# A fused attention and ternary feed-forward block: a second buffer for P's 512-column tiles, AV one slot later, and ternary weights cast by GpSimd's transfers

## The chip, the cores and the metric

The kernel runs on one core of one Trainium2 chip. The metric is the device time of one execution in microseconds (us). The kernel before was timed three times; its profile comes from one further execution.

## The reference

The input x has 16 batches of 512 rows and 512 columns, in float32. Attention and feed-forward work side by side on the same normalised rows:

```python
xn = layernorm(x)                                   # over the 512 columns
# attention, 16 heads of 32
qkv = xn @ w_qkv.T + b_qkv                          # 1536 x 512 weights
scores = q @ k.T / sqrt(32) + causal mask
out = softmax(scores) @ v
attn = out @ w_out.T + b_out
# feed-forward, 1408 hidden columns, ternary weights (-1, 0, 1)
g = (xn @ gate_w.T) * gate_s
u = (xn @ up_w.T) * up_s
ffn = ((silu(g) * u) @ down_w.T) * down_s
result = x + attn + ffn
```

## The kernel before

All products run in fp16. A float32 value that needs more precision is split in two fp16 parts, a high part and the rest ("low"), and the products of the parts are summed. The ternary weights are exact in fp16 and have one part.

**Slots.** The heads are worked on in groups of four (G, 64 groups in all, four to a batch b). A group has U = 10 slots, so a batch has 40 and the whole run has 640, numbered n. A slot has one unit of scores: one head's 512-column tile of query rows (units 0, 1, 5, 6), or two smaller tiles. Each engine has its own program, a list in this order of slots, and takes its instructions strictly in that order. What is to be done in a slot besides the scores stands in tables: `av_at`, `qk_at`, `v_at`, `o_at`, `d_at`, `f_at`, `norm_at`.

**A unit's path.** TensorE writes the scores to one of four PSUM banks in slot n (`scores`). VectorE masks them and takes the maximum (`maximum`, L588). ScalarE takes the exponential (`exponent`, L500). Two slots later ScalarE writes the high part of P (`high`, L492), and VectorE the low part (`low`, L598), both to a buffer `phl[qt]` that is chosen by the tile's width, 128(qt+1) columns. `scores(n)` waits for `low(n-4)`, since it takes the same bank. SyncE then transposes the buffer to `pt` by a DMA (`turn_p`, L954); there is one such DMA for each half p of a group (heads 0 and 1, heads 2 and 3) and each width, eight in a group. `high` of a tile waits for the transposition of the previous contents of its buffer (`d_pt[qt]`). There is one buffer for each width, so the 512-column tiles of slots 5 and 6 wait for the transposition of slots 0 and 1, which SyncE starts in slot 5.

**AV.** `av(G)` has 48 products of the transposed P with v. It stands in slot 4 of the next group, behind that slot's scores (`av_at`, AV_K = 4). It waits for all eight transpositions. ScalarE drains it one slot later to `q32[0]` (`drain_av`, L468); GpSimd splits that to the two parts of `att` (`split_av`, L791 and L793; in GpSimd's list of a slot it stands ahead of `residual`, `down_add`, `split_hidden` and `load_xin`). After a batch's last group the four products with w_out follow: `o(b, t)` in slots 47, 48, 49 and 51 counted from the batch's first slot, that is, slots 7, 8, 9 and 11 of the next batch. They wait for `p_al`, the end of `split_av`.

**Feed-forward.** `gate_up(f)` writes a tile of g and u to one bank; ScalarE, VectorE (L608, L613) and GpSimd (`split_hidden`, L804, L808, L810) make the hidden tile of it. There are 22 a batch; `F_WIN` says in which slots. The first group of a batch (but for batch 0) has them in slots 2, 2, 4 and 5. `down_product` runs in slots 19, 21, 37, 39; VectorE scales its result to `dtmp` (L632), GpSimd adds that to `res` (L820).

**Weights before.** `w_qkv` comes in 12 chunks, the ternary gate, up and down in 33 (11 each). Each chunk is 128 x 512 float32, 256 KB. SyncE issues all 45 as plain DMAs to 15 staging slots that lie in buffers not yet in use (`res`, `att`, `xnT[1]`, parts of `ht`, `dtmp`), by a planner: `slot_of`, `w_load`, `w_slot`. ScalarE (17 ternary chunks, L434) or GpSimd (16, L764) copies a chunk to fp16. 18 chunks are issued ahead of the first slot and the others in the first 20 slots, in SyncE's queue between `stack` and `turn_p`.

**Normalisation.** GpSimd loads a tile of x to `xin` (L838) four slots ahead of its statistics (L562). VectorE scales it to `xs32` (L572), GpSimd takes the high part (L908), VectorE the low part (L737).

Of the kernel before, what the change touches and what calls it, by code (L numbers as in the profile page):

```python
# [5 lines left out]
ACT = mybir.ActivationFunctionType  # L6
# [21 lines left out]
U = 10  # L28
# [38 lines left out]
def fast_path(nc, ctx, B, x, w_qkv, b_qkv, w_out, b_out, gate, up, down, gate_s, up_s, down_s, out):  # L67
# [33 lines left out]
    phl = [sb(f"phl{i}", [128, 2, 2, 128 * (i + 1)], F16) for i in range(4)]  # L101
# [22 lines left out]
    d_w = [sem(f"d_w{i}") for i in range(15)]  # L124
# [4 lines left out]
    d_pt = [sem(f"d_pt{i}") for i in range(4)]  # L129
# [16 lines left out]
    AV_K, QK_K = 4, (3, 6)  # L146
# [15 lines left out]
    av_at = {U * (G + 1) + AV_K: G for G in range(NGRP)}  # L162
# [13 lines left out]
    later = [(n - 4, ("norm", *v)) for n, v in norm_at.items()] + [(n - 3, ("check", c)) for n, c in check_at.items()]  # L176
    for n, what in sorted(later + [(n - 3, ("wout", k)) for n, k in wout_at.items()]):
        i = what[-1] % 2
        xin_load_at[n] = what
        xin_turn[what] = 1 + sum(x[-1] % 2 == i for x in xin_turn)  # L180
        xin_free[what] = xin_reader[i]
        xin_reader[i] = {"norm": (v_xs, 4 * what[1] + what[-1] + 1), "check": (a_ms, what[1] + 1), "wout": (v_wo, what[1] + 1)}[what[0]]
# [36 lines left out]


    pair = lambda t, i: t[:, 2 * i:2 * i + 2, :].rearrange("p a b -> p (a b)").bitcast(F32)
    stage = [(res[i][:, :], 16 + i) for i in range(4)]
    stage += [(pair(att[:, i // 2], i % 2), 15) for i in range(4)]
    stage += [(pair(xnT[1], i), 8) for i in range(4)]
    stage += [(x0[2], 15), (x0[3], 20), (dtmp[:, :], 20)]
    flat = lambda w: w.rearrange("p a b -> p (a b)")
    chunks, w_slot = [], []

    def qkv_chunk(n, m):
        chunks.append(("split", ("wqkv", m), w_qkv[m], flat(wqkv[:, 0, m]), flat(wqkv[:, 1, m])))  # L230
        w_slot.append(n)

    def gate_up_chunks(n, i):
        chunks.append(("act", ("wg", i), gate[i], flat(wg[:, i]), None))
        chunks.append(("pool", ("wu", i), up[i], flat(wu[:, i]), None))
        w_slot.extend((n, n))

    def down_chunk(n, i):
        chunks.append(("pool" if i % 2 else "act", ("wd", i), down[i], wd[:, i], None))
        w_slot.append(n)  # L240

    for m in (8, 9, 0, 4, 1, 5, 10, 11):
        qkv_chunk(-1, m)
    gate_up_chunks(-1, 0)
    qkv_chunk(-1, 2)
    qkv_chunk(-1, 6)
    for n, i in ((-1, 1), (1, 2), (2, 3), (4, 4), (5, 5), (6, 6), (8, 7)):
        gate_up_chunks(n, i)
    qkv_chunk(9, 3)
    gate_up_chunks(10, 8)  # L250
    down_chunk(10, 0)
    qkv_chunk(11, 7)
    gate_up_chunks(12, 9)
    down_chunk(12, 1)
    gate_up_chunks(13, 10)
    for n, i in ((13, 2), (13, 3), (14, 4), (14, 5), (15, 6), (15, 7), (16, 8), (16, 9), (18, 10)):
        down_chunk(n, i)
    W_FIRST, W_EARLY = w_slot.index(1), 18
    NCH = len(chunks)
    slot_of, before = [], []  # L260
    for n in range(NCH):
        last = lambda i: max([m for m in range(n) if slot_of[m] == i], default=-1)
        free = [i for i in range(len(stage)) if stage[i][1] > w_slot[n] and (n >= 12 or i < 12)]
        slot_of.append(min(free, key=lambda i: (last(i), i)))
        before.append(last(slot_of[n]))
    turn_of = [slot_of[:n].count(slot_of[n]) for n in range(NCH)]
    slot_last = [max(n for n in range(NCH) if slot_of[n] == i) for i in range(len(stage))]
    stage = [buf for buf, n in stage]
    w_load = [max([w_slot[n] - 4, 0] + [w_slot[before[n]] + 1] * (before[n] >= 0)) for n in range(NCH)]


    on_act = [sum(c[0] != "pool" for c in chunks[:n + 1]) for n in range(NCH)]
    on_pool = [sum(c[0] == "pool" for c in chunks[:n + 1]) for n in range(NCH)]
    lows = [sum(c[0] == "split" for c in chunks[:n + 1]) for n in range(NCH)]
    finished = [{"split": (v_w, lows[n]), "act": (a_w, on_act[n]), "pool": (p_w, on_pool[n])}[c[0]] for n, c in enumerate(chunks)]
    ready = {c[1]: finished[n] for n, c in enumerate(chunks)}
# [8 lines left out]
    def tensor_program(eng):  # L285
# [42 lines left out]
        def av(G):  # L328
            b, g = divmod(G, 4)
            for qt in range(4):  # L330
                w.wait_ge(d_pt[qt], 16 * (2 * G + 2))
# [95 lines left out]
    def scalar_program(eng):  # L427
        w = Waits(eng)

        def weight(n):  # L430
            kind, key, src, hi, lo = chunks[n]
            if kind != "pool":
                w.wait_ge(d_w[slot_of[n]], 16 * (turn_of[n] + 1))
                eng.activation(hi, stage[slot_of[n]], ACT.Copy, scale=WS if kind == "split" else 1.0).then_inc(a_w, 1)  # L434
# [42 lines left out]
        def high(n):  # L477
# [5 lines left out]
            for j, qt, off in segs(u):  # L483
                w.wait_ge(d_pt[qt], 16 * (2 * G + j // 2))
# [5 lines left out]
            for k, (j, qt, off) in enumerate(segs(u)):  # L490
                c, W = 2 * (n % NSTAT) + k, 128 * (qt + 1)
                i = eng.activation(phl[qt][:, j % 2, 0], pb[:, off:off + W], ACT.Copy, scale=st_r[:, c:c + 1])  # L492
# [11 lines left out]
        for t in range(4):  # L504
            hl = xhl[t][:, 0] if t < 2 else phl[3][:, t - 2, 0]
# [8 lines left out]
        for n in range(8, 11):  # L514
            weight(n)
        drain_qk(0, 1)
        weight(11)
        v_high(0, 0, 1)
        for n in range(12, W_FIRST):
            weight(n)  # L520
# [4 lines left out]
        for n in range(LAST):  # L525
# [16 lines left out]
            for i in range(W_FIRST, NCH):  # L542
                if w_slot[i] == n:
                    weight(i)


    def vector_program(eng):
        w = Waits(eng)

        def weight_low(n):  # L550
            kind, key, src, hi, lo = chunks[n]
            if kind == "split":
                w.wait_ge(a_w, on_act[n])
                eng.scalar_tensor_tensor(lo, stage[slot_of[n]], WS, hi, ALU.mult, ALU.subtract).then_inc(v_w, 1)  # L554
# [13 lines left out]
        def scaled(i, t, xs, xi):  # L568
            st = lst[t]
            w.wait_ge(v_xl, i if i > 4 else 0)  # L570
            w.wait_ge(p_rs, i + 1)
            eng.tensor_scalar(xs, xi, st[:, 6:7], st[:, 8:9], op0=ALU.subtract, op1=ALU.mult).then_inc(v_xs, 1)  # L572
# [20 lines left out]
        def low(n):  # L593
            pb = bank[n % NSB]
            w.wait_ge(a_hi, n + 1)
            for k, (j, qt, off) in enumerate(segs(n % U)):
                c, W = 2 * (n % NSTAT) + k, 128 * (qt + 1)
                i = eng.scalar_tensor_tensor(phl[qt][:, j % 2, 1], pb[:, off:off + W], st_r[:, c:c + 1], phl[qt][:, j % 2, 0],  # L598
# [16 lines left out]
        def v_low(b, hf, tp):  # L615
            psum = job_bank["v", b, hf, tp][:, :].rearrange("p (a f) -> p a f", a=2)
            part = lambda p: vv[:, p, 2 * tp:2 * tp + 2, 256 * hf:256 * hf + 256]
            w.wait_ge(a_vh, 4 * b + 2 * hf + tp + 1)
            eng.scalar_tensor_tensor(part(1), psum, QS / (XS * WS), part(0), ALU.mult, ALU.subtract).then_inc(v_vl, 1)
# [7 lines left out]
        def down_scale(b, t):  # L627
            w.wait_ge(p_set, 9)
            w.wait_ge(*finished[slot_last[14]])
            w.wait_ge(p_dy, 4 * b + t)  # L630
# [605 lines left out]
```

## Time and profile before

| | |
|---|---|
| median of 3 runs | 1947.92 us (1947.15 to 1948.87) |
| profiled execution | 1948.99 us, with a span of 1947.2 us |
| TensorE busy (matmul) | 1866.0 us, 96% of the span |
| VectorE, ScalarE, GpSimd busy | 1504.4, 1450.8, 1255.8 us |
| mean granted TensorE clock | 0.99 of full speed |

The span runs from the first instruction to the last. An engine's busy time is a union of its instructions, so a matmul that is queued behind another counts once. "L588" is line 588 of the kernel before. PE is TensorE, DVE VectorE, ACT ScalarE, POOL GpSimd; SPq is SyncE's queue of DMA issues. All of TensorE's products have one line, L287, so they are told apart by their tiles (`bank<-pt,vv` is AV, `bank<-wout,att` the product with w_out, `bank<-stk` the scores).

### The profile page before, as it was taken

What the parts mean: (1) busy time and instruction counts of PE and PEld (TensorE: products, weight loads), DVE (VectorE), ACT (ScalarE), POOL (GpSimd) and SP (SyncE); (2) the same over time, 40 slices, a digit from 0 to 9 for tenths busy, and PEclk for the clock granted to TensorE, in tenths of its full rate; (3) what the DMA queues carried; (4) which work ended last, traced back from release to release, by engine and by line L of the source; (5) the groups of instructions that cost most, each with busy time, mean ns of one, the idle gap of its engine ahead of it and who ended that gap; (6) DMA issues with size and microseconds to landing.
All of it is one profiled execution on the core that took longest, in us unless ns stands there. A gap on an engine that the chain in (4) does not pass through costs nothing.

```text
span 1947.2 us, 44190 instructions
## 1 busy us (share of the span) xinstructions
PE 1866.0 (96%) x14978; PEld 1222.0 (63%) x14978; DVE 1504.4 (77%) x4516; ACT 1450.8 (75%) x4280; POOL 1255.8 (64%) x1800
## 2 busy tenths in 40 slices
PE   6689999999999999999999999999999999999997
PEld 4456566665766666566666756666566666756663
DVE  4677778777787877878778787877878777787884
ACT  4677687867778787787877778777787777777683
POOL 4676666857577585776857576575666656576462
PEclk9899999999999999999999999999999999999998
DMA  7997978889798796978889798786968878797674
GB/s 217 216 171 141 185 134 182 159 151 184 134 191 144 159 182 127 205 139 170 166 144 193 136 178 138 156 168 122 198 129 169 144 142 175 135 187 129 122 157 94
DMA packets 818839, 310.26 MB, mean 159 GB/s; under 512 B 756464, under 2 KB 789232, under 8 KB 818608
## 3 DMA queue, kind: packets, MB, share of 16 engines
q1 hardware_dynamic: 800928, 249.44, 70.9%
q0 software_dynamic: 17680, 57.95, 10.4%
q8 instruction: 119, 1.95, 0.4%
q14 instruction: 112, 0.92, 0.2%
HBM read 55.59 MB, written 16.78 MB: 37 GB/s over the span
## 4 chain that ended last, share of the span: by engine, by line
PE 70%; DVE 9%; DMA 6%; SPq 6%; ACT 5%; issue 3%; POOL 2%; POOLq 0%; ACTq 0%; DVEq 0%
PE bank L287 70%; DMA pt<-phl 5%; SPq L947 4%; DVE phl L598 3%; ACT phl L492 2%; DVE bank L588 1%; SPq L954 1%; ACT bank L500 1%; DVE res L625 1%; DVE small L562 1%; DVE xhl L737 1%; ACT small L488 0%; SPq L939 0%; DMA xnT<-in_up_dram 0%; DVE ft L608 0%
## 5 line engine op out<-in xcount | busy, mean ns | idle before, releaser
L598 DVE SCALAR_TENSOR_TENSOR phl<-bank,small,phl 128x512 f16<-128x512 f32 (+3 forms) x1024 | 526.6, 546 | 187.9 <-ACT phl L492 184.9
L500 ACT ACTIVATE bank<-bank,small 128x512 f32<-128x512 f32 (+3 forms) x1024 | 516.0, 505 | 167.2 <-DVE small L588 166.4
L588 DVE CUSTOM_DVE_ANT_0 bank<-bank,mask 128x512 f32<-128x512 f32 (+3 forms) x1024 | 484.3, 504 | 162.8 <-PE bank L287 160.4
L492 ACT ACTIVATE phl<-bank,small 128x512 f16<-128x512 f32 (+3 forms) x1024 | 500.0, 531 | 91.6 <-DMA pt<-phl 81.0
L287 PE MATMUL bank<-xnT,wg 128*128 128x256 f16 x2816 | 367.8, 273 | 6.5 <-DVE fh L613 4.8
L287 PE MATMUL bank<-xnT,wu 128*128 128x256 f16 x2816 | 367.4, 274 | 0.0
L287 PE MATMUL bank<-xnT,wqkv 128*128 128x512 f16 x1536 | 352.4, 379 | 1.1 <-ACT q L461 1.1
L287 PE MATMUL bank<-wd,ht 128*128 128x512 f16 x1408 | 317.5, 381 | 4.0 <-POOL ht L810 2.1
L287 PEld LDWEIGHTS bank<-xnT,wg 128*128 128x128 f16 x2816 | 264.0, 98 | 68.9 <-issue 5.9
L287 PEld LDWEIGHTS bank<-xnT,wu 128*128 128x128 f16 x2816 | 276.6, 98 | 33.0
L287 PE MATMUL bank<-stk 96*128 96x512 f16 (+3 forms) x1024 | 245.8, 301 | 26.6 <-DVE phl L598 25.2
L810 POOL TENSOR_TENSOR ht<-fh,ht 128x256 f16<-128x256 f32 x352 | 238.4, 677 | 29.4
L287 PEld LDWEIGHTS bank<-xnT,wqkv 128*128 128x128 f16 x1536 | 147.8, 98 | 167.2 <-issue 1.7
L804 POOL TENSOR_TENSOR fh<-fh,ft 128x256 f32<-128x256 f32 x176 | 127.6, 725 | 188.9 <-DVE ft L608 188.8
L287 PEld LDWEIGHTS bank<-wd,ht 128*128 128x128 f16 x1408 | 137.2, 98 | 162.8 <-issue 4.1
L450 ACT ACTIVATE ft<-bank,small 128x256 f32<-128x256 f32 x352 | 169.6, 483 | 77.8 <-PE bank L287 77.6
L808 POOL TENSOR_SCALAR ht<-fh 128x256 f16<-128x256 f32 x352 | 143.2, 407 | 130.6 <-DVE fh L613 114.1
L500 ACT ACTIVATION_READ_ACCUMULATOR bank<-bank,small 128x1 f32 x1024 | 216.0, 211 | 0.0
L287 PE MATMUL bank<-wqkv,xnT 128*128 128x256 f16 x1536 | 180.6, 275 | 14.1 <-DMA xnT<-xhl 14.1
L820 POOL TENSOR_TENSOR res<-res,dtmp 128x512 f32<-128x512 f32 x64 | 81.1, 1268 | 155.7 <-DVE dtmp L632 155.5
L287 PE MATMUL bank<-wout,att 128*128 128x512 f16 x768 | 177.5, 381 | 3.7 <-POOL att L793 2.9
L287 PEld LDWEIGHTS bank<-wqkv,xnT 128*128 128x128 f16 x1536 | 150.4, 98 | 38.9 <-DVE wqkv L554 14.0
(110 smaller groups left out, 2195.6 us busy)
## 6 DMA issues: line engine op xcount, KB each, us to landing
stk<-qkp SPq DMA_DIRECT2D x768, 64.0 KB, 2.1
res<-in_x_dram POOLq DMA_DIRECT2D x64, 256.0 KB, 4.7
xin<-in_x_dram POOLq DMA_DIRECT2D x60, 256.0 KB, 4.6
out_dram<-res POOLq DMA_DIRECT2D x60, 256.0 KB, 3.7
pt<-phl SPq DMA_TRANSPOSE x512, 4.2
xin<-in_gate_dram POOLq DMA_DIRECT2D x11, 256.0 KB, 3.5
xin<-in_up_dram POOLq DMA_DIRECT2D x11, 256.0 KB, 3.3
xin<-in_down_dram POOLq DMA_DIRECT2D x11, 256.0 KB, 3.5
```

Source lines behind the costliest of these rows:

```text
L287: mm = lambda o, lhs, rhs, start, stop, **k: eng.matmul(o, lhs, rhs, start=start, stop=stop, skip_group_check=True, **k)
L450: eng.activation(ft[f % 3][:, :], bank[4 + f % 2][:, 0:256], ACT.Tanh, scale=gsh[:, k:k + 1]).then_inc(a_ft, 1)
L492: i = eng.activation(phl[qt][:, j % 2, 0], pb[:, off:off + W], ACT.Copy, scale=st_r[:, c:c + 1])
L500: i = eng.activation(pb[:, off:off + W], pb[:, off:off + W], ACT.Exp, bias=st_m[:, c:c + 1], scale=-1.0, accum_out=st_s[:, c:c + 1])
L562: eng.bn_stats(st[:, 0:6], xi).then_inc(v_bn, 1)
L588: i = eng.tensor_tensor_reduce(out=bk[:, off:off + W], in0=bk[:, off:off + W], in1=mask[:, 512 - W:512], scale=-(32.0 ** -0.5) / (QS * QS) ...
L598: i = eng.scalar_tensor_tensor(phl[qt][:, j % 2, 1], pb[:, off:off + W], st_r[:, c:c + 1], phl[qt][:, j % 2, 0], ALU.mult, ALU.subtract)
L804: eng.tensor_tensor(hh[:, :], hh[:, :], ft[f % 3][:, :], ALU.mult).then_inc(p_fm, 1)
L808: eng.tensor_scalar(hs[:, 0], hh[:, :], 1.0, 1.0, op0=ALU.mult, op1=ALU.mult).then_inc(p_hh, 1)
L810: eng.tensor_tensor(hs[:, 1], hh[:, :], hs[:, 0], ALU.subtract).then_inc(p_fl, 1)
L820: eng.tensor_tensor(res[t][:, :], res[t][:, :], dtmp[:, :], ALU.add).then_inc(p_dy, 1)
L947: eng.dma_start(stk[G % 2][32 * blk:32 * blk + 32, j], qkp[G % 2][32 * j:32 * j + 32, a:a + step + 1:step, :]).then_inc(d_stk[2 * (G % 2) ...
```

## The change

Three edits are made together.

1. `phl[3]` becomes two buffers, one for each half of a group, each with its own semaphore (`d_pt[3][p]`). `high` of a 512-column tile now waits for the transposition of the same half of the group before. AV_K goes from 4 to 5 (the last group's AV stays in slot 4), and `turn_p(G, 0, 3)` from slot 5 to slot 6 of SyncE's list.
2. The ternary weights are no longer staged. GpSimd issues 15 DMAs that read float32 and write fp16 straight into `wg`, `wu` and `wd`: two of one chunk, ten of two chunks, three of three or four chunks. Six of them come as soon as the fourth tile of batch 0's x is transposed (`d_xT[3]`), ahead of `split_qk(0, 0)`; two behind `split_qk(0, 1)`; four behind `split_qk(1, 1)`; the three of `wd` in slots 1, 3 and 5. The copies on ScalarE and GpSimd are gone. All 12 chunks of w_qkv are now loaded and split ahead of slot 0.
3. To make room, `dtmp` becomes `q32[0]`, the buffer to which AV is drained, with two new waits (`drain_av` for earlier `down_add`, `down_scale` for earlier `split_av`); `xs32` is gone and the scaled tile stays in `xin`, so that `xin` is free two slots later, and its loads are issued three slots ahead of the statistics in place of four.

```diff
-    phl = [sb(f"phl{i}", [128, 2, 2, 128 * (i + 1)], F16) for i in range(4)]
+    phl = [[sb(f"phl{i}", [128, 2, 2, 128 * (i + 1)], F16)] for i in range(3)]
+    phl.append([sb(f"phl3_{p}", [128, 2, 2, 512], F16) for p in range(2)])
...
-    dtmp = sb("dtmp", [128, 512], F32)
+    dtmp = q32[0]
-    xs32 = sb("xs32", [128, 512], F32)
...
-    AV_K, QK_K = 4, (3, 6)
+    AV_K, QK_K = 5, (3, 6)
...
-    av_at = {U * (G + 1) + AV_K: G for G in range(NGRP)}
+    av_at = {U * (G + 1) + (AV_K if G < NGRP - 1 else 4): G for G in range(NGRP)}
+    avs_ahead = {bt: sum(n < m for n in av_at) for m, bt in d_at.items()}
+    ds_ahead = {G: sum(n < m for n in d_at) for m, G in av_at.items()}
...
-    later = [(n - 4, ("norm", *v)) for n, v in norm_at.items()] + ...
+    later = [(n - (4 if n < 4 else 3), ("norm", *v)) for n, v in norm_at.items()] + ...
...
+    chunks = (8, 9, 0, 4, 1, 5, 10, 11, 2, 6, 3, 7)
+    ffn_loads, ffn_sem = [], {}
+    for lo, hi in ((0, 1), (1, 3), (3, 5), (5, 7), (7, 9), (9, 11)):
+        ffn_loads += [("wg", lo, hi), ("wu", lo, hi)]
+    ffn_loads += [("wd", 0, 4), ("wd", 4, 8), ("wd", 8, 11)]
+    for i, (name, lo, hi) in enumerate(ffn_loads):
+        for k in range(lo, hi):
+            ready[name, k] = (d_ffn[i], 16)
+    ffn_load_at = {1: (12,), 3: (13,), 5: (14,)}
...
         def drain_av(G):
             g = G % 4
             w.wait_ge(p_al, G)
+            w.wait_ge(p_dy, ds_ahead[G])
...
             for j, qt, off in segs(u):
-                w.wait_ge(d_pt[qt], 16 * (2 * G + j // 2))
+                w.wait_ge(*((d_pt[3][j // 2], 16 * G) if qt == 3 else (d_pt[qt][0], 16 * (2 * G + j // 2))))
...
         def down_scale(b, t):
             w.wait_ge(p_dy, 4 * b + t)
+            w.wait_ge(p_al, avs_ahead[b, t])
...
+        def load_ffn(i):
+            name, lo, hi = ffn_loads[i]
+            if name == "wd":
+                dst = wd[:, lo:hi]
+            else:
+                dst = {"wg": wg, "wu": wu}[name][:, lo:hi].rearrange("p k a b -> p k (a b)")
+            eng.dma_start(dst, {"wg": gate, "wu": up, "wd": down}[name][lo:hi].rearrange("k p f -> p k f")).then_inc(d_ffn[i], 16)
...
-        for n in range(10):
-            weight(n)
+        w.wait_ge(d_xT[3], 16)
+        for i in range(6):
+            load_ffn(i)
         split_qk(0, 0)
         split_qk(0, 1)
-        for n in range(10, W_FIRST):
-            weight(n)
+        load_ffn(6)
+        load_ffn(7)
         split_qk(1, 0)
         split_qk(1, 1)
+        for i in range(8, 12):
+            load_ffn(i)
...
-                if k == 5:
-                    turn_p(G, 0, 3, n - 4)
                 if k == 6:
+                    turn_p(G, 0, 3, n - 5)
                     turn_p(G, 0, 2, n - 3)
                     turn_p(G, 0, 0, n - 3)
...
-            for i in range(W_EARLY, NCH):
-                if w_load[i] == n:
-                    load_weight(i)
```

## Rows read from the trace of the kernel before

**Rows 1.** Busy time by stage: stretch, its length, engines, TensorE clock, DMA share, GB/s

```profile
36.60:80.00 43.40, 33.62 (x236) 23.47 (x236) 35.19 (x103) 35.24 (x98) 28.84 (x48) 0.92 0.98 224
80.00:91.14 11.14, 3.32 (x48) 1.89 (x49) 1.12 (x4) 2.47 (x8) 3.38 (x5) 0.55 1.10 214
91.14:130.00 38.86, 34.73 (x253) 21.14 (x250) 25.29 (x75) 26.44 (x76) 28.58 (x37) 0.91 0.92 182
130.00:169.50 39.50, 37.51 (x294) 24.58 (x292) 30.88 (x96) 33.03 (x99) 27.02 (x40) 1.00 0.78 145
...
406.40:1811.30 1404.90, 1386.72 (x11233) 913.04 (x11232) 1112.38 (x3353) 1071.56 (x3182) 932.78 (x1333) 1.00 0.83 158
```

**Rows 2.** Waits of TensorE from 130 to 1860 us: total, times, longest

```profile
PE bank L287 <- DVE phl L598: 17.8, 16, 3.1
PE bank L287 <- issue: 5.5, 8, 1.4
PE bank L287 <- POOL ht L810: 2.1, 3, 1.0
```

**Rows 3.** Waits of TensorE in the first 130 us

```profile
PE bank L287 <- ACT wd L434: 1.9, 1, 1.9
```

**Rows 4.** The chain that ended last, around a stall at 695 us: start, length

```profile
689.06 5.43 DMA pt<-phl
...
696.04 63.96 PE bank L287 x504
```

**Rows 5.** Timeline of TensorE in the head: the first AV

```profile
87.82 3.39 PE L287 MATMUL bank<-pt,vv 128*32 128x512 f16 x48 [11.61 <-DMA pt<-phl]
```

**Rows 6.** Timeline of SyncE's queue ahead of the first AV

```profile
79.75 4.13 SPq L954 DMA_TRANSPOSE pt<-phl  x1
```

**Rows 7.** Timeline, slots 44 to 47: a batch's last AV and first product with w_out

```profile
181.98 1.81 PE L287 MATMUL bank<-pt,vv 128*32 128x512 f16 x48
183.73 1.05 PE L287 MATMUL bank<-xnT,wg 128*128 128x256 f16 x8
...
185.70 1.04 PE L287 MATMUL bank<-xnT,wg 128*128 128x256 f16 x8
...
190.48 1.89 PE L287 MATMUL bank<-wout,att 128*128 128x512 f16 x8
...
186.47 0.69 ACT L468 ACTIVATE q<-bank,small 128x512 f32<-128x512 f32 x1
...
187.19 0.41 DVE L608 SCALAR_TENSOR_TENSOR ft<-ft,bank 128x256 f32<-128x256 f32 x1
...
187.95 1.15 POOL L793 TENSOR_TENSOR att<-q,att 128x512 f16<-128x512 f32 x1
189.06 0.73 POOL L804 TENSOR_TENSOR fh<-fh,ft 128x256 f32<-128x256 f32 x1
...
190.36 0.67 POOL L810 TENSOR_TENSOR ht<-fh,ht 128x256 f16<-128x256 f32 x1
```

**Rows 8.** The same two instructions in the last of the 15 batches that have them

```profile
1829.79 1.16 POOL L793 TENSOR_TENSOR att<-q,att 128x512 f16<-128x512 f32 x1
...
1832.33 1.89 PE L287 MATMUL bank<-wout,att 128*128 128x512 f16 x8
```

**Rows 9.** Durations by line: ns min/median/max

```profile
L434 ACT ACTIVATE wg<-att x4: 635/648/673, 52.7 to 78.0; 128x512 f16<-128x512 f32 x4
...
L838 POOL DMA_DIRECT2D xin<-in_x_dram x60: 584/611/763, 37.4 to 1719.1; - x60
```

**Rows 10.** DMA rate from 20 to 30 us, 40 slices of 0.25 us

```profile
GB/s 90 107 131 90 131 238 262 279 270 238 328 311 320 279 426 402 410 401 402 418 402 393 393 402 401 401 402 393 385 393 393 303 238 246 246 229 164 25 0 0
```

**Rows 11.** The start of the first group: GpSimd, TensorE and the first statistics from `xin`

```profile
19.13 5.61 PE L287 MATMUL bank<-xnT,wqkv 128*128 128x512 f16 x24
...
25.23 0.62 POOL L780 TENSOR_SCALAR qkp<-q 128x512 f16<-128x512 f32 x1
...
47.42 0.61 DVE small L562
```

More of the change, by code:

```diff
@@ L123, in fast_path @@
     d_small = [sem(f"d_small{i}") for i in range(5)]
-    d_w = [sem(f"d_w{i}") for i in range(15)]
+    d_w = [sem(f"d_w{i}") for i in range(12)]
+    d_ffn = [sem(f"d_ffn{i}") for i in range(15)]
     d_x0 = [sem(f"d_x0{i}") for i in range(4)]
@@ L221, in fast_path @@
     pair = lambda t, i: t[:, 2 * i:2 * i + 2, :].rearrange("p a b -> p (a b)").bitcast(F32)
[L222 to L225, printed above, removed]
+    stage = [res[i][:, :] for i in range(4)]
+    stage += [pair(att[:, i // 2], i % 2) for i in range(4)]
+    stage += [pair(xnT[1], i) for i in range(4)]
+    part = lambda qt, j: phl[qt][j // 2 if qt == 3 else 0]
@@ L226, in fast_path @@
     flat = lambda w: w.rearrange("p a b -> p (a b)")
[L227 to L240, printed above, removed]
@@ L258, in fast_path @@
-    W_FIRST, W_EARLY = w_slot.index(1), 18
-    NCH = len(chunks)
[L260 to L275, printed above, removed]
@@ L276, in fast_path @@
-    ready = {c[1]: finished[n] for n, c in enumerate(chunks)}
+    chunks = (8, 9, 0, 4, 1, 5, 10, 11, 2, 6, 3, 7)
+    NCH = len(chunks)
+    ready = {("wqkv", m): (v_w, n + 1) for n, m in enumerate(chunks)}
+    ffn_loads, ffn_sem = [], {}
[5 more added lines that the diff above has]
+            ready[name, k] = (d_ffn[i], 16)
@@ L430, in weight @@
         def weight(n):
[L431 to L434, printed above, removed]
+            w.wait_ge(d_w[n], 16)
+            eng.activation(flat(wqkv[:, 0, chunks[n]]), stage[n], ACT.Copy, scale=WS).then_inc(a_w, 1)
         def wout_high(k):
@@ L504, in scalar_program @@
         for t in range(4):
-            hl = xhl[t][:, 0] if t < 2 else phl[3][:, t - 2, 0]
+            hl = xhl[t][:, 0] if t < 2 else phl[3][0][:, t - 2, 0]
             w.wait_ge(v_xs, t + 1)
@@ L513, in scalar_program @@
         drain_qk(0, 0)
-        for n in range(8, 11):
-            weight(n)
+        weight(8)
         drain_qk(0, 1)
+        weight(9)
+        v_high(0, 0, 1)
+        weight(10)
         weight(11)
-        v_high(0, 0, 1)
-        for n in range(12, W_FIRST):
-            weight(n)
         drain_qk(1, 0)
@@ L687, in first_low @@
         def first_low(t):
-            hl = xhl[t][:, :, :] if t < 2 else phl[3][:, t - 2]
+            hl = xhl[t][:, :, :] if t < 2 else phl[3][0][:, t - 2]
             w.wait_ge(a_xh, t + 1)
@@ L708, in vector_program @@
         v_low(0, 0, 0)
-        for n in range(7, W_FIRST):
+        for n in range(7, 10):
             weight_low(n)
         v_low(0, 0, 1)
+        for n in range(10, 12):
+            weight_low(n)
         for f in range(F_FIRST):
@@ L907, in gpsimd_program @@
                 w.wait_ge(v_xs, i + 1)
-                eng.tensor_scalar(xhl[t % 2][:, 0], xs32[:, :], 1.0, 1.0, op0=ALU.mult, op1=ALU.mult).then_inc(p_xh, 1)
-            for i in range(W_FIRST, NCH):
-                if w_slot[i] == n:
-                    weight(i)
+                eng.tensor_scalar(xhl[t % 2][:, 0], xin[t % 2][:, :], 1.0, 1.0, op0=ALU.mult, op1=ALU.mult).then_inc(p_xh, 1)
+            for i in ffn_load_at.get(n, ()):
+                load_ffn(i)
             if n in xin_load_at:
@@ L932, in turn_x @@
             if b == 1:
[L933 to L934 removed]
+                w.wait_ge(v_w, NCH)
             if b >= 2:
@@ L964, in sync_program @@
         for t in range(4):
-            turn_x(0, t, xhl[t] if t < 2 else phl[3][:, t - 2])
+            turn_x(0, t, xhl[t] if t < 2 else phl[3][0][:, t - 2])
             load_weight(4 + t)
@@ L968, in sync_program @@
             eng.dma_start(dst[:, :], src.to_broadcast([128, 512])).then_inc(d_small[i + 3], 16)
-        for n in range(8, W_EARLY):
+        for n in range(8, NCH):
             load_weight(n)
```

86 lines of the change are left out of this document (25 added, 61 removed).

## The prediction

> **What bounds the kernel now.** I read the stages first, then what TensorE waits for, then the timeline around the longest waits and around the instructions that the change moves.
>
> The stages [rows 1] show two regimes. From 406 to 1811 us, twelve batches, TensorE is busy for 1386.7 of 1404.9 us at a full clock. Nothing but its own work bounds it there, and all that any edit can win in these twelve batches is 18.2 us. A batch takes 117.1 us, a slot 2.93. In the first batch it is otherwise. TensorE idles for 9.8, 7.8, 4.1 and 2.0 us in the four stretches from 36.6 to 169.5 us, 23.7 us in all, and its clock is granted at 0.92, 0.55 and 0.91 in the first three. At half clock (1.2 GHz in place of 2.4) the first AV takes 3.39 us [rows 5] and a later one 1.81 [rows 7].
>
> The waits tell what the idle time is. After 130 us they come to 25.4 us [rows 2]. Most is `scores` waiting for VectorE's low part of P, which frees the bank. The chain shows where this comes from: a transposition `pt<-phl` runs from 689.06 to 694.49, and TensorE goes on at 696.04, behind one high and one low part [rows 4]. I read this as a 512-column tile that waits for its single buffer. The 5.5 us "issue" are, by their place ahead of AV, AV's wait for the last transpositions, which the profile does not name. In the head the largest wait is the first AV's, 11.6 us for transpositions [rows 5]. SyncE's queue issued the last of them only at 79.75, and spent 4.1 us on it [rows 6], between weight loads. 1.9 us are a wait for a ternary weight's copy [rows 3].
>
> **Part 1, later batches: the second buffer and the later AV.** The waits that they aim at are 25.4 us [rows 2], less the 2.0 us that fall between 130 and 169.5 us [rows 1], which I count in the head: 23.4. A buffer's transposition now has ten slots and not five before the next tile needs it, so the waits for the low part should go. AV gets one slot, about 2 us of TensorE's work, against waits of at most 1.4 us, so these go as well. The three transpositions of a group's first half are now issued one behind another in slot 6, and the narrower ones may hold a tile now and then. I take a gain of 20, with bounds of 14 (the low-part waits only in part) and 23.4.
>
> **What the later AV queues up.** AV of a batch's last group stands now in slot 45 of its 40 and has to pass through `drain_av`, `split_av` and then the product with w_out, in slot 47. Before, the split ends at 187.95 + 1.15 = 189.10 and the product starts at 190.48 [rows 7]: a distance of 1.38 us. In the last batch it is 1830.95 to 1832.33, again 1.38 [rows 8], and the 15 batches are alike. The product itself isn't moved: AV and one slot's other work change places. AV starts later by what it moves behind, 185.70 - 183.73 = 1.97 us [rows 7]. If the chain behind it merely shifted by this, TensorE would wait 1.97 - 1.38 = 0.6 us in each of 15 batches, 9 us.
>
> But the chain sits in lists. On ScalarE the drain goes one slot down, behind the next exponential. 2.93 us after the end of 187.16 it had is 190.1, and with the 1.9 us of the split (187.2 to 189.10) that is 192.0. On GpSimd `split_hidden` of slot 44 now comes ahead of the split. It can begin when L608 ends, at 187.60, and takes 1.97 us (189.06 to 191.03) [rows 7]; so does a `load_xin`, now in this very slot (three ahead of the statistics in slot 48), 0.61 us [rows 9]; with the split this is 187.6 + 2.0 + 0.6 + 1.9 = 192.1. The two agree on about 192.0, a wait of 1.5 us after 190.48. 15 times this is 22.5 us. The upper bound is 2.2 us each, 33 in all: the three pieces on GpSimd again, with 0.6 us for work beside them that slows them. I take 22.5. Nothing covers it: no `gate_up` stands in slots 46 to 49, and TensorE is in order.
>
> **Part 2, the head.** Removed: 17 copies of 0.65 us on ScalarE [rows 9] and 16 on GpSimd, and 33 loads from SyncE's list. Nearly all of them lie in the stretch from 36.6 to 110 us.
>
> - 36.6 to 80 us, without the AV wait (which has 3.8 of the 9.8 us): 6.0 us of idle time and up to 3.5 us of clock (0.08 of 43.4). VectorE is busy for 35.2 of 43.4 us there [rows 1], does as much as before except for two low parts of w_qkv, and its work comes in a chain with ScalarE's. I take 4.
> - The AV wait: 11.6 us and 1.6 of clock, 13.2. Without the loads between them the transpositions are issued when their tiles are ready, and AV has one slot more. I take 12.5.
> - 91 to 130 us: 4.1 us idle, of which 1.9 for the weight copy [rows 3], and up to 3.5 of clock. I take 5.5.
> - 130 to 169.5 us: 2.0 idle, I take 1.3.
> - The start. TensorE needs all four transposed tiles at 19.13, so GpSimd can issue from then at the latest [rows 11]. Six issues with ten chunks cost between 6 and 10 times 0.61 us [rows 9]: 3.7 to 6.1 us, so `split_qk(0, 0)` is free at 22.8 to 25.2, against 25.23 before. I take a gain of 1.
>
> Sum 24.3, with bounds of 14 and 30. The transfers: 22 chunks and 11 later ones, the same 8.7 MB read as before, and the plain loads reached about 400 GB/s [rows 10], 0.65 us a chunk. The trace has no casting transfer. From below I set this same rate, from above the rate at which it starts to hurt (third rival), and I take a rate near the plain one.
>
> **Part 3, the shared buffers.** `down_scale` of slots 19, 21, 37, 39 and AV's drain of slots 16, 26, 36, 46 are at least one slot apart in each direction, so I cost the two new waits at nothing; each would show as VectorE or ScalarE waiting for GpSimd. `xin`'s load is issued 2.93 us later in a lead of four slots; at a landing time of some 4.6 us (page, DMA issues) there remain 3 x 2.9 - 4.6 = 4 us, less GpSimd's lag. Nothing. If this cover were gone VectorE would stand still ahead of everything else in its slot.
>
> One rule of the skill speaks against part 2. The 60 issues of `xin<-in_x` on GpSimd, beside a busy VectorE, took 584 to 763 ns [rows 9]; none was held up, and with 0.76 us each the six ahead of `split_qk(0, 0)` would take 4.6 us. The Trainium skill (SBUF — State Buffer, the box on the "DVE blocks DMA" trap) says that GpSimd cannot write descriptors while VectorE runs an operation that holds the shared port pair, and gives some 3.1 us in place of 0.62. By that estimate the six issues would take 18.6 us and the sum would be 12 us higher.
>
> **The sum.** 1948.99 (the profiled execution) - 20 - 24.3 + 22.5 = 1927.2 us. The profiled execution is 1.1 us above the median, so the prediction for the median is **1926 us**, 1.1% faster. The tail (AV of the last group stays in slot 4) is left as it is.
>
> **Rivals.**
>
> 1. *The wait for `split_av` is short.* GpSimd and ScalarE, freed of their other waits, run the chain at its mere shift: 0.6 us in each of 15 batches, 9 us. The time is 1926 - 13.5 = 1912, from 1904 to 1917. For it speaks that the shift by itself is only 1.97 us; against it that two lists give the same 1.5 us by separate ways. Chance 0.22.
> 2. *The buffer does not do what it says.* The waits move from the 512-column tile to the narrower ones behind it, as three transpositions now start together. The 20 us stay, the w_out wait comes on top: 1946 us. For it speaks a transposition of 5.4 us in a slot of 2.9 [rows 4]; against it that only tiles of slots 7 and later wait for these. Chance 0.08.
> 3. *Slower: the casting transfers are slow.* Its place is VectorE's first statistics from `xin`, at 47.42 [rows 11]. This load is now in the same queue behind 22 chunks. 23 x 0.262 MB from 19.1 to 47.4 us is 213 GB/s; below this rate VectorE stands still and with it everything. At 120 GB/s it lands 22 us late and the gain is gone; at 100 GB/s it lands 32 us late and the kernel takes 1958 us. Against it speaks the 400 GB/s of plain loads [rows 10], twice the rate from which it starts. Chance 0.07.
> 4. *GpSimd's issues are held up by VectorE.* The place is the start: `split_qk(0, 0)`, and with it the first scores, come later by what six issues take over 6.1 us; from 10 us late on it would show as such, 1937 us. Against it stands the longest issue, 0.76 us [rows 9]; for it the rule named above. Chance 0.03.
>
> My forecast has 0.55, and 0.05 is left for what I don't see. Its own range is 1917 to 1937. The range for 8 in 10 takes in most of rival 1 below and nearly reaches rival 2 above: 1908 to 1943. A measurement of this kernel tells 0.2% (3.9 us) from no change. Faster than that are the forecast, rival 1, rival 4 and a part of the rest: 0.81; rival 2 gives half of its chance and some of the rest to "same", 0.08; rival 3 and the remainders are slower, 0.11.
>
> **What would show it.** In the profile after: L492 no longer waits for `pt<-phl` at 512 columns; AV has no "issue" wait; a new wait of TensorE for POOL's `att` ahead of `bank<-wout,att`, 15 times near 1.5 us; the first AV's wait below 1 us and a clock of 1.00 from 60 to 130 us; the casting loads landing in under 10 us and their issues at 0.6 to 1.2 us. The prediction is wrong if the wait for `att` is far from 1.5 us, or if VectorE, at 35.2 of 43.4 us, holds the head where it is.

## The result, and the profile after

The changed kernel takes 1961.8 us in the median of four runs (1959.1 to 1967.0); the kernel before, on the same chip, 1947.5 (1944.8 to 1948.9). The ratio is 1.0066, with an interval of 1.0044 to 1.0089: slower by 0.7% where 1.1% faster was forecast, and outside the range of 1908 to 1943. The profiled execution took 1966.95 us, with a span of 1963.4, so its ledger is made against the 1947.2 us of the span before.

Time by slot says where it went. The start of a slot's first scores product, in us from the start of the span, in both traces:

| slot | 0 | 14 | 16 | 20 | 26 | 40 | 600 | end |
|---|---|---|---|---|---|---|---|---|
| before | 36.60 | 75.83 | 94.95 | 111.72 | 129.22 | 169.46 | 1811.30 | 1947.2 |
| after | 36.56 | 74.02 | 80.39 | 92.69 | 117.66 | 157.84 | 1831.41 | 1963.4 |

The first batch ends 11.6 us earlier, the fourteen batches to slot 600 take 31.7 us longer (1673.6 in place of 1641.8), and the tail 3.9 us less. 31.7 - 11.6 - 3.9 = 16.2.

Busy time by stage in the kernel after, the same stretches as [rows 1] and the same columns:

```profile
36.60:80.00 43.40, 37.85 (x314) 27.45 (x315) 34.92 (x105) 31.38 (x95) 27.98 (x43) 0.96 1.08 182
80.00:91.14 11.14, 8.97 (x56) 5.10 (x54) 9.88 (x31) 8.80 (x26) 9.87 (x15) 1.00 1.07 162
91.14:130.00 38.86, 33.78 (x250) 20.96 (x249) 25.40 (x73) 25.86 (x78) 26.04 (x35) 0.91 0.88 164
130.00:169.50 39.50, 38.56 (x305) 25.68 (x304) 30.14 (x92) 30.18 (x90) 20.09 (x29) 1.00 0.69 136
...
406.40:1811.30 1404.90, 1363.31 (x10985) 893.58 (x10984) 1091.65 (x3290) 1048.59 (x3122) 930.22 (x1314) 1.00 0.81 156
```

From 80 to 91 us TensorE works where it stood still before. But from 91 to 130 us it idles for 5.1 us (4.1 before) at the same clock of 0.91, and in the long last stretch its idle time has risen from 18.2 to 41.6 us. The waits of TensorE in the kernel after, from 170 to 1860 us (total, times, longest), show with what:

```profile
PE bank L252 <- POOL att L754: 27.8, 14, 2.5
PE bank L252 <- DVE phl L558: 13.8, 16, 2.9
PE bank L252 <- DVE fh L573: 5.9, 9, 1.1
PE bank L252 <- POOL ht L771: 0.2, 1, 0.2
```

The first is the forecast wait of the product with w_out, 2.0 us each. The "issue" waits of AV are gone, and so are the stalls of slot 19, which made up most of the old wait for the low part [rows 2]. But the line `phl L558` has 9.2 us, and `fh L573` 5.9, that the kernel before did not have. Put down to slots, they lie in slot 15 of all 14 batches and in slot 34 of nine. Both stand right behind the place from which AV was taken: `scores(15)` followed the AV of slot 14, and the gate/up product of slot 34 followed the AV of the same slot.

The other 4.6 us of `phl L558` are in slot 21 of two batches. There a narrower tile waits for its transposition; the worse of the two, ScalarE and then TensorE:

```profile
1060.57 0.84 ACT L458 ACTIVATE phl<-bank,small 128x384 f16<-128x384 f32 x2 [6.94 <-DMA pt<-phl]
1062.37 0.39 PE L252 MATMUL bank<-stk 96*128 96x512 f16 x1 [2.86 <-DVE phl L558]
```

A slot 14 with what follows it, TensorE and the low part, in the timeline (start, duration, engine, operation, and in brackets the idle time before). First the kernel before:

```profile
446.16 1.81 PE L287 MATMUL bank<-pt,vv 128*32 128x512 f16 x48 [0.56 <-issue]
...
449.67 0.38 PE L287 MATMUL bank<-stk 96*128 96x512 f16 x1
...
447.86 0.74 DVE L598 SCALAR_TENSOR_TENSOR phl<-bank,small,phl 128x512 f16<-128x512 f32 x1
```

Then the same slots of the kernel after:

```profile
436.75 0.38 PE L252 MATMUL bank<-stk 96*128 96x256 f16 x2
436.97 1.04 PE L252 MATMUL bank<-xnT,wg 128*128 128x256 f16 x8
437.85 1.04 PE L252 MATMUL bank<-xnT,wu 128*128 128x256 f16 x8
439.84 0.38 PE L252 MATMUL bank<-stk 96*128 96x512 f16 x1 [0.96 <-DVE phl L558]
440.18 1.81 PE L252 MATMUL bank<-pt,vv 128*32 128x512 f16 x48
```

```profile
438.95 0.74 DVE L558 SCALAR_TENSOR_TENSOR phl<-bank,small,phl 128x512 f16<-128x512 f32 x1
```

`scores(15)` takes the bank that `low(11)` frees at 439.69. TensorE reaches it at 438.88. Before, the 1.81 us of AV stood in between and covered this: the bank was free at 448.60 and TensorE came to `scores(15)` at 449.67. Now AV starts 0.34 us behind the scores. In slot 34 it is the gate/up product that comes too early, for VectorE's `fh`:

```profile
497.37 1.05 PE L252 MATMUL bank<-xnT,wg 128*128 128x256 f16 x8 [1.12 <-DVE fh L573]
```

### The profile page after: what moved, and what is told of

Read it like the earlier page. It is cut to its first block, busy times and chain, and to the rows that moved or that the text cites. A ratio compares the mean times of both kernels' runs of the same rounds, so it can differ in the third digit from the quotient of the medians.

```text
span 1963.4 us, 44220 instructions
## 1 busy us (share of the span) xinstructions
PE 1867.7 (95%) x14978; PEld 1220.6 (62%) x14978; DVE 1503.8 (77%) x4516; ACT 1439.7 (73%) x4263; POOL 1269.1 (65%) x1799
## 4 chain that ended last, share of the span: by engine, by line
PE 60%; DVE 16%; ACT 10%; POOL 6%; issue 4%; DMA 2%; SPq 1%; POOLq 0%; ACTq 0%; DVEq 0%
PE bank L252 60%; DVE phl L558 5%; ACT phl L458 4%; DVE bank L548 3%; ACT bank L466 2%; DVE res L585 2%; DVE small L523 2%; POOL att L754 2%; DMA pt<-phl 1%; DVE xhl L700 1%; DVE ft L568 1%; ACT ft L415 1%; POOL ht L771 1%; POOL fh L765 1%; POOL att L752 1%
## 5 line engine op out<-in xcount | busy, mean ns | idle before, releaser
L558 DVE SCALAR_TENSOR_TENSOR phl<-bank,small,phl 128x512 f16<-128x512 f32 (+3 forms) x1024 | 525.9, 545 | 159.0 <-ACT phl L458 154.4
L781 POOL TENSOR_TENSOR res<-res,q 128x512 f32<-128x512 f32 x64 | 80.9, 1265 | 135.0 <-DVE q L592 134.8
```

What stands on the lines that cost most here:

```text
L558: i = eng.scalar_tensor_tensor(part(qt, j)[:, j % 2, 1], pb[:, off:off + W], st_r[:, c:c + 1], part(qt, j)[:, j % 2, 0], ALU.mult, ALU.sub ...
L781: eng.tensor_tensor(res[t][:, :], res[t][:, :], dtmp[:, :], ALU.add).then_inc(p_dy, 1)
```

## What the forecast wait consists of

The timeline of the kernel after in slots 124 to 127, against [rows 7]:

```profile
413.69 0.41 DVE L568 SCALAR_TENSOR_TENSOR ft<-ft,bank 128x256 f32<-128x256 f32 x1
...
414.24 0.72 POOL L765 TENSOR_TENSOR fh<-fh,ft 128x256 f32<-128x256 f32 x1 [0.66 <-DVE ft L568]
...
414.89 0.69 ACT L434 ACTIVATE q<-bank,small 128x512 f32<-128x512 f32 x1
415.06 0.40 POOL L769 TENSOR_SCALAR ht<-fh 128x256 f16<-128x256 f32 x1
...
415.54 0.67 POOL L771 TENSOR_TENSOR ht<-fh,ht 128x256 f16<-128x256 f32 x1
...
416.15 0.61 POOL L799 DMA_DIRECT2D xin<-in_x_dram  x1
...
416.80 0.63 POOL L752 TENSOR_SCALAR att<-q 128x512 f16<-128x512 f32 x1
...
417.51 1.40 POOL L754 TENSOR_TENSOR att<-q,att 128x512 f16<-128x512 f32 x1
...
418.97 2.76 PE L252 MATMUL bank<-wout,att 128*128 128x512 f16 x12 [1.82 <-POOL att L754]
```

ScalarE has drained AV at 415.58, but GpSimd begins to split it only at 416.80: `split_hidden` and the load of x stand ahead of it, and GpSimd has no gap over 0.1 us from 414.24 to 417.43. That is the second of the prediction's two lists, piece by piece. ScalarE's list is 1.2 us ahead of it and does not bind. From the end of L568 (414.10) to the end of the split it is 4.81 us, for the 4.5 of the working; 0.24 of this is L754, 1.40 in place of 1.16. Nine of the 14 waits are 1.81 to 1.82 us, two 2.0 and 2.1, and three 2.41 to 2.51. Ahead of these three, and of no other, VectorE has one more instruction in its list, the reduction of L606 (0.67 us, at 534.8, 894.8 and 1255.8), and L568, where this chain starts, comes behind it. The fifteenth, ahead of the last batch, where no further x is to be loaded, is 0.1.

## The experiments

Each kernel is given as its difference from the kernel after, unless said otherwise, and each ratio is to the kernel before on the same chip in the same series. The kernel before took 1952.0 us (median of 25 runs, 1940.5 to 1965.2) in the first series, 1951.0 in the second, 1949.7 in the third, so small steps are read from ratios and from waits in the traces and not from absolute times. The means of a batch are those of batches 2 to 14, from the start of their first scores: 117.07 us before, 119.59 after.

**First series.** Theory: AV's later slot costs more than the second buffer and the head give, by GpSimd's list. Rivals: the weight loads, or the second buffer itself.

*AV back in slot 4.*

```diff
-    AV_K, QK_K = 5, (3, 6)
+    AV_K, QK_K = 4, (3, 6)
```

> The changed kernel with AV back in slot 4, all else kept. My theory: the loss comes from AV's later slot, through three waits of TensorE per batch that the trace after shows (the product with w_out about 2.0 us and now and then a stretch at half clock behind it, the scores of slot 15 about 0.7, gate_up in slot 34 about 0.5), against some 0.5 us of AV's own waits that come back. That is about 3.1 us in each of 15 batches: 1962 - 46 = 1916 us, from 1908 to 1924, and no wait for POOL's att but in the tail. Rival: the casting transfers, the shared buffers or the new order of transpositions slow the later batches; then this kernel stays above 1950.

Measured: 1932.6 us, ratio 0.9892 (0.982 to 0.9963), a mean batch of 116.98 us. The waits of TensorE from 170 to 1880 us:

```profile
PE bank L252 <- issue: 8.1, 11, 2.6
PE bank L252 <- POOL ht L771: 6.0, 10, 1.0
PE bank L252 <- DVE phl L558: 5.1, 9, 1.1
```

All three new waits are gone, and one constant turns 0.7% slower into 1.1% faster. The size expected (1908 to 1924) was too good. The stall in slot 19, which the second buffer removes (15.9 us before, 0.6 here), comes back in part: the down product of the same slot now waits for `split_hidden` (6.0 us), and AV for transpositions (8.1, for 4.8 before). A batch is 0.1 us shorter than before, and no more.

*AV in slot 4 for a batch's last group alone.*

```diff
-    av_at = {U * (G + 1) + (AV_K if G < NGRP - 1 else 4): G for G in range(NGRP)}
+    av_at = {U * (G + 1) + (4 if G % 4 == 3 else AV_K): G for G in range(NGRP)}
```

> The changed kernel with AV back in slot 4 for the last group of each batch alone (the one that the product with w_out waits for), in slot 5 for the three others. If the w_out wait is the main cost and local to this AV: about 2.45 us in each of 15 batches go, 1962 - 37 = 1925 us (1919 to 1932), the scores' wait in slot 15 and gate_up's in slot 34 stay. If the waits come from AV's place in all groups alike, most of the loss stays: above 1945.

Measured: 1940.4 us, 0.9939 (0.9907 to 0.997), a mean batch of 117.72, between the two forecasts. The wait for `att` is gone from the batches, but this kernel is not the faster of the two (its ten runs, from 1936.8 us on, all lie above the four of the first, up to 1935.7):

```profile
PE bank L252 <- DVE phl L558: 18.5, 16, 1.6
PE bank L252 <- DVE fh L573: 6.0, 9, 1.1
```

17.9 of the 18.5 us are in slot 15 (9.2 in the kernel after): I read this as the wait for `att` having hidden part of it, which was not tested. So the later AV has a price of its own in the groups in which nothing waits for `split_av`.

*Without the second buffer.* `phl[3]` is one buffer with one semaphore again, AV_K is 4, and `turn_p(G, 0, 3)` is in slot 5. What is left of the change is the casting loads and the shared buffers.

```diff
-    phl.append([sb(f"phl3_{p}", [128, 2, 2, 512], F16) for p in range(2)])
+    phl.append([sb("phl3", [128, 2, 2, 512], F16)])
...
-    AV_K, QK_K = 5, (3, 6)
+    AV_K, QK_K = 4, (3, 6)
```

> The changed kernel with AV in slot 4, one buffer for the 512-column tiles and the transposition of the first half in slot 5, as before; so the casting transfers and the shared buffers alone. Theory: they give the 11.6 us that the trace after is ahead at slot 40 and nothing later: 1947.5 - 11.6 = 1936 us (1931 to 1941), some 18 us above the kernel with AV in slot 4 and two buffers; the waits of L458 for pt<-phl are back. Rival: the second buffer is worth nothing, then both are equal within 4 us.

Measured: 1943.9 us, 0.9958 (0.9922 to 0.9993), a mean batch of 117.72, with 14.3 us of waits in slot 19 and 8.3 at AV in slot 14. The loads and the shared buffers together help a little; they are not what makes the kernel slower. Between this kernel and the first lies the second buffer, 0.7% by the medians, but the intervals overlap (the runs themselves do not: 1936.2 us and more against 1935.7 and less). The shared buffers were not taken out by themselves. In the kernel after, the waits that the prediction named as their sign do not appear: from 170 to 1860 us VectorE waits for TensorE and ScalarE alone, never for `xin`'s load or for GpSimd, and ScalarE never at AV's drain.

*`split_av` ahead of `split_hidden`.* `split_hidden` of slot 44 is held back until GpSimd has split the batch's last AV.

```diff
+        held = ()
...
+            for f in held:
+                split_hidden(f)
+            held = ()
...
-            for f in f_at.get(n - 1, ()):
-                split_hidden(f)
+            if n in av_at and av_at[n] % 4 == 3 and av_at[n] < NGRP - 1:
+                held = f_at.get(n - 1, ())
+            else:
+                for f in f_at.get(n - 1, ()):
+                    split_hidden(f)
```

> The changed kernel, but on GpSimd split_hidden of slot 44 goes behind split_av of the batch's last group. Theory: GpSimd's list sets the end of the split. In the trace after ScalarE's drain ends at 415.5 and the split starts at 416.8, so 1.2 to 1.3 us of the w_out wait go in each of 15 batches: it falls from 1.9 to 0.6 us, and the time to 1962 - 19 = 1943 us (1938 to 1950). Rival: ScalarE's list binds; the wait stays at 1.5 us or more and the time above 1955.

Measured: 1943.5 us, 0.9942 (0.9911 to 0.9973). The wait of TensorE from 170 to 1860 us:

```profile
PE bank L252 <- POOL att L754: 8.2, 14, 1.0
```

14 waits of 0.59 us, for 14 of 1.99. GpSimd's list is shown to be what held the product. 0.6 us is also what the first rival of the prediction gave for the mere shift. The waits of slot 15 (9.3) and slot 34 (5.9) stay.

**Second series.** What does AV's slot cost by itself, does a later w_out product cover the wait, and does the place of the 512-column tile's transposition matter?

*The kernel after once more.*

> The changed kernel once more, beside the other kernels of this call, as their common measure. 1.005 to 1.01 of the kernel before; the same three waits per batch (w_out about 1.9 us in slot 7, the scores of slot 15, gate_up of slot 34).

Measured: 1962.8 us, 1.0063 (1.0031 to 1.0095), as before. Its trace has the same waits (28.1 us for `att`, 9.3 in slot 15, 6.0 in slot 34) with a span of 1952.4. It had no stretch at half clock between 101.1 and 1940 us. The first profiled execution of the kernel after had three there, from 105.4, 542.3 and 1262.5. The wait in slot 21 is 0.3 us here, for 4.6 there.

*The kernel before with AV_K = 5 alone* (one buffer, staged weights, `turn_p` in slot 5; the last group's AV stays in slot 4).

> The kernel before with AV in slot 5 and nothing else changed (weights staged, one buffer, the transposition of the first half in slot 5 of SyncE's list, where it now stands ahead of AV's end). Theory: AV's slot alone brings the loss: the w_out wait of 0.6 us or more in each of 15 batches, and since the single buffer waits for a transposition that itself waits for AV, more at slot 19. 1948 + 30 to 45: ratio 1.015 to 1.023. Rival: AV's slot costs only together with the casting transfers or the new buffers; then the ratio is under 1.005.

Measured: 2010.4 us, 1.0306 (1.0243 to 1.0369): 59 us more than before, for the 30 to 45 expected. The rival is out. The waits of TensorE from 170 to 1900 us:

```profile
PE bank L287 <- DVE phl L598: 36.7, 25, 6.6
PE bank L287 <- POOL att L793: 15.0, 14, 1.5
PE bank L287 <- DVE res L625: 12.9, 12, 2.3
PE bank L287 <- DVE fh L613: 6.1, 10, 1.1
```

They come to 71 us, for 24 before. The wait for `att` is 1.07 us each and not 1.99: this kernel loads x four slots ahead, so I take it that the 0.61 us of its issue are not in the way here; L793 takes 1.15 us in place of 1.40. 13.8 us are in slot 15, 6.1 in slot 34. The stall in slot 19 has grown from 15.9 to 23.1: with one buffer the later AV makes it worse. So the later AV costs without the other edits too: 59 us, for the 31 that it costs with them (below).

*The w_out products one slot later*, in slots 48 to 51.

```diff
-            for t, k in enumerate((47, 48, 49, 51)):
+            for t, k in enumerate((48, 49, 50, 51)):
```

> The changed kernel (AV in slot 5) with the four products with w_out in slots 8, 9, 10, 11 in place of 7, 8, 9, 11. If these products stand too close behind AV, the 27.9 us of waits for POOL's att go with this edit too: 1962 - 28 = 1934, ratio to before 0.99 to 0.997, and the waits of slots 15 and 34 stay. Rival: the wait follows to slot 8, or another takes its place in slots 7 to 11, since the queue and not the distance binds; the ratio stays above 1.003.

Measured: 1968.7 us, 1.01 (1.0048 to 1.0152), no better than the kernel after. By slots, 15.3 us are left of the wait for `att`, and two come in its place, 11.2 us of w_out in slot 10 for VectorE's `res` and 7.3 of the scores in slot 8. Moving the consumer one slot does not cover this wait here; it hands it on.

*AV in slot 4, and the transposition `turn_p(G, 0, 3)` back in slot 5*, with two buffers and the casting loads.

```diff
-    AV_K, QK_K = 5, (3, 6)
+    AV_K, QK_K = 4, (3, 6)
...
+                if k == 5:
+                    turn_p(G, 0, 3, n - 4)
                 if k == 6:
-                    turn_p(G, 0, 3, n - 5)
```

> AV in slot 4, two buffers, casting transfers, and the transposition of the first half back in slot 5 of SyncE's list. With it in slot 6 the kernel with AV in slot 4 gained nothing in the later batches over one buffer as before: AV's own waits in slot 14 were 7.8 us in place of 3.2. Theory: these come from transpositions that are issued later, one behind another; with this edit AV's waits fall to 3 to 4 us and the time by 4 to 8 us, to a ratio of 0.982 to 0.988. Rival: they come from TensorE being earlier, not from SyncE's list; then nothing changes, 0.988 to 0.992.

Measured: 1931.6 us, 0.9902 (0.9861 to 0.9943). With the first experiment's 0.9892 beside it, the place of this transposition makes no difference that these runs can tell. Against the kernel after on the same chip it is 1962.8 - 1931.6 = 31 us: the price of AV's slot, with all of the change kept but the place of that transposition. The waits tell the same: TensorE's come to 47.7 us in the kernel after (170 to 1860 us) and to 16.8 here (170 to 1880), 30.9 less.

**Third series.** TensorE stands still ahead of the first scores, in a stretch in which the casting loads move data. The timeline of TensorE in the kernel after:

```profile
31.80 1.04 PE L252 MATMUL bank<-xnT,wu 128*128 128x256 f16 x8
36.56 0.39 PE L252 MATMUL bank<-stk 96*128 96x512 f16 x1 [3.73 <-DMA stk<-qkp]
36.79 4.45 PE L252 MATMUL bank<-wqkv,xnT 128*128 128x256 f16 x24
41.08 0.38 PE L252 MATMUL bank<-stk 96*128 96x512 f16 x1
41.30 2.78 PE L252 MATMUL bank<-wqkv,xnT 128*128 128x256 f16 x24
```

The wait was 1.0 us before, and from 37.1 to 40.5 us, behind it, the granted clock is 0.5, its lower level of 1.2 GHz: the same 24 products take 4.45 us and then 2.78. The experiment is the last kernel with two loads moved behind `split_qk(1, 1)` and four more into slots 1 and 3, and those of `wd` later by four slots:

```diff
-        load_ffn(6)
-        load_ffn(7)
         split_qk(1, 0)
         split_qk(1, 1)
-        for i in range(8, 12):
-            load_ffn(i)
+        load_ffn(6)
+        load_ffn(7)
...
-    ffn_load_at = {1: (12,), 3: (13,), 5: (14,)}
+    ffn_load_at = {1: (8, 9), 3: (10, 11), 5: (12,), 7: (13,), 9: (14,)}
```

> The kernel with AV in slot 4 and the transposition back in slot 5, with GpSimd's casting loads spread: the seventh and eighth behind split_qk(1, 1), the next four in slots 1 and 3, those of wd in slots 5, 7 and 9. The traces with casting loads have TensorE waiting 3.0 to 4.0 us for stk<-qkp ahead of the first scores (1.0 before) and a stretch at half clock from 37 us on. Theory: the casting loads share the DMA engines with these transfers and make them late; with fewer in flight the wait falls to about 1.5 us, the half-clock stretch at 37 us goes, and slot 2 is reached 2 to 4 us earlier. The time moves by no more than that: ratio to before 0.986 to 0.991. Rival: the wait is GpSimd's own lateness in split_qk; then the first scores stay at 37 us or later.

Measured: 1935.2 us, 0.9937 (0.991 to 0.9964). At the start it does what the theory says:

```profile
34.98 0.39 PE L252 MATMUL bank<-stk 96*128 96x512 f16 x1 [0.87 <-DMA stk<-qkp]
```

The scores start at 34.98 in place of 37.55 in the kernel that it was made from. The rival, that GpSimd itself is late, does not fit: it ends `split_qk(0, 1)`, for which the stacking copies wait, at 27.70 and 28.18, so from there to the scores it is 7.3 us and 9.4. None of this reaches the end: 0.9937 against 0.9902, intervals overlapping. The first AV waits 2.7 us for its transpositions again, and slot 40 starts at 158.8.

## Why the prediction was wrong

The ledger of the profiled executions, terms as predicted (-21.8 us in all) and as measured (+16.2):

| term | predicted | measured |
|---|---|---|
| later batches: waits for the low part, AV, down product | -20 | -19.2 |
| w_out waits for `split_av` | +22.5 | +27.8 |
| `scores(15)` and `gate_up` in slot 34 | 0 | +15.1 |
| later batches, rest | 0 | +8.0 |
| head | -24.3 | -11.6 |
| tail | 0 | -3.9 |

The first line is 24.0 us of waits in batches 1 to 14 before, less the 4.6 and 0.2 of the kernel after. The rest is 31.7 + 19.2 - 27.8 - 15.1. It is not idle time: TensorE's busy time in batches 1 to 14 is 1617.9 us before, 1625.7 after and 1622.4 in the repeated profile of the same kernel. The first of the two profiles has two stretches at half clock there, of 3.4 us each, behind w_out waits at 542 and 1262 us; the repeated one has none, and that is about the 3.3 us between them. Where the other 4.4 us come from is open.

The forecast and the ledger are 38 us apart. The line of `scores(15)` and slot 34 is the largest part with 15.1 us, the head comes next with 12.7, then the rest with 8.0 and the w_out wait with 5.3. So the step below is the largest that failed, and it does not explain the whole distance.

**The step that failed** is the costing of AV's later slot by what comes behind AV alone ("The product itself isn't moved: AV and one slot's other work change places"). It asked who waits for AV's result and not what AV's 1.81 us had been covering in the slot that it left. Slot 14 without AV is shorter than the chain that frees the bank of `scores(15)`, and slot 34 likewise for a gate/up bank. Both waits were costed at nothing and named nowhere, and together they are 15.1 us. The AV waits of at most 1.4 us [rows 2] that the later slot was to remove came to 5.0. With the old slot restored both waits are gone, and with the w_out wait gone too the kernel is 31 us faster. With AV in slot 4 for the last group alone both stay (17.9 and 6.0 us).

**Right, and nearly the right size: the w_out wait.** Mechanism, place and count hold, GpSimd's list included; 14 times 1.99 where 15 times 1.5 was taken. The mean is within the bound of 2.2; three of the waits, of 2.4 to 2.5, are above it. The longer part is the slower L754 and, in those three, VectorE's reduction ahead of the chain.

**Right in its own place, given back elsewhere: the second buffer.** The stall in slot 19 went, as did AV's wait, and ScalarE has no wait for the transposition of a 512-column tile left. Where AV stays in slot 4, most of the gain is lost again at the down product and at AV: a batch is 116.98 us for 117.07 before. Measured against the kernel with one buffer and the other edits kept (117.72) it is 0.7 us a batch, though that profile has 6.8 us at half clock in a later batch. The prediction's own bound was 18.2 us in twelve batches, 1.5 us a batch; with 20 us it took nearly all of it.

**Half right: the head.** Of the 24.3 us forecast 11.6 came. By the slots of the table: the start 0.0 (predicted 1), slots 0 to 14 gain 1.8 (4), the AV wait 12.8 (12.5), slots 16 to 26 lose 3.0 (5.5 gained), slots 26 to 40 gain 0.1 (1.3). The AV wait was sized well. At the start GpSimd ended `split_qk(0, 1)` at 27.16 us for 30.61 before, more than was forecast, but the slower stacking copies used this up. The rest was counted as if idle time vanished with the copies of the weights. In slots 16 to 26 other waits stand in their place. TensorE in the kernel after:

```profile
85.75 0.39 PE L252 MATMUL bank<-stk 96*128 96x384 f16 x2 [2.17 <-DVE phl L558]
...
95.92 0.39 PE L252 MATMUL bank<-stk 96*128 96x512 f16 x1 [1.09 <-DVE phl L558]
...
103.94 0.39 PE L252 MATMUL bank<-stk 96*128 96x384 f16 x2 [0.92 <-DVE phl L558]
106.51 1.87 PE L252 MATMUL bank<-xnT,wqkv 128*128 128x512 f16 x4 [2.17 <-DMA xnT<-xhl]
```

and SyncE's queue there:

```profile
93.56 8.25 SPq L912 DMA_TRANSPOSE pt<-phl  x1
101.85 2.00 SPq L897 DMA_TRANSPOSE xnT<-xhl  x1
```

One transposition held SyncE's queue for 8.25 us, the next one behind it was issued at 101.85, and TensorE waited for it from 104.3 to 106.5; from 105.4 to 112.2 its granted clock is 0.5. Why that transposition took 8.25 us was not tested; loads of `res` run beside it. Over all kernels with the casting loads slot 40 starts between 154.4 and 162.4 us, a scatter of 8 us that no edit here explains. The head's gain is therefore 7 to 15 us in single profiles, and what sets it is open.

**The rivals.** The first (a short wait) did not happen, but its 0.6 us is what the reordered list gives. The second (the waits move to the narrower tiles) is refuted as the main course by slot 19, but its mechanism does act now and then, as the prediction's part 1 allowed: ScalarE waits for transpositions at 384 columns in slots 19 and 20, up to 6.9 us, and TensorE's stall in slot 21 comes of it, 4.6 us in two of 14 batches in one profile and 0.3 in the other. The third and fourth (slow casting transfers, issues held up) are refuted by the loads themselves, here the three instruction groups in the kernel after (ns min/median/max) and their landing:

```profile
L726 POOL DMA_DIRECT2D wg<-in_gate_dram x6: 716/744/788, 18.1 to 35.3; - x6
L726 POOL DMA_DIRECT2D wu<-in_up_dram x6: 548/726/741, 18.9 to 36.0; - x6
L726 POOL DMA_DIRECT2D wd<-in_down_dram x3: 814/817/819, 39.3 to 55.1; - x3
...
DMA to landing us min/median/max: 4.9/8.4/12.0
```

The first six take 4.2 us (18.11 to 22.27), for the estimate of 3.7 to 6.1, and VectorE never waits for `xin`. The 3.1 us of the Trainium skill (SBUF — State Buffer, "A bandwidth-pool intuition that's wrong", below the box on the "DVE blocks DMA" trap) are given there for a DMA issued by GpSimd beside a VectorE `tensor_copy`; the prediction read them as the time of an issue. No issue here is near that; VectorE was busy for only 1.4 of those 4.2 us, so the rule was not put to a hard test there. The slower side was given 0.11, and to mechanisms that had no part in it: none of the rivals named the cover that AV took with it.

**Which version is best.** AV in slot 4 with both other edits, 0.9892 and 0.9902 of the kernel before, ahead of the kernel before by about 1% and of the kernel after by 1.6 to 1.7%. These runs tell neither the two from one another nor the kernel with the spread loads from them.

## What to carry to other kernels

Before an instruction is moved out of a slot, ask of the slot that it leaves what its time was covering: list each wait that ends within its duration behind it, here a PSUM bank four slots back. Then follow the result down each in-order list that it passes, piece by piece; that part of the method gave the right place and nearly the right size. A gain read from idle time where all engines are busy needs the name of what arrives late next; without it, here, half of the sum came.

## What the runs showed of the hardware

- A casting transfer, float32 in DRAM to fp16 in SBUF, cost GpSimd 0.76 us (the very first) and 0.55 to issue for one chunk of 128 x 512, 0.72 to 0.79 for two, and 0.82 for three or four: less than in proportion. The stacking copies beside them were late: TensorE's wait for `stk` was 2.8 to 4.0 us with all twelve loads of `wg` and `wu` there, 0.9 with six of the twelve moved back, and 1.0 in the kernel before.
- GpSimd's subtraction on 128 x 512 (L754) took 1.16 us in the median and up to 1.49; ahead of the w_out product it took 1.39 to 1.40 in 13 of 14 batches, where the kernel before has 1.15 to 1.16 in all. Why was not tested.
- Behind the w_out waits of 1.8 to 2.5 us the granted clock fell to 0.5 for 3.4 us in two of 14 cases, behind waits of 2.41 and 2.51 us, and not behind a third of 2.41. The twelve products then took 4.36 and 4.45 us in place of 2.76. In a second execution of the same kernel, with waits of up to 2.53 us, it fell behind none.
- One DMA transposition held SyncE's queue for 8.25 us, where the median of 512 is 1.62.
